# Sort of 100,000 edges: key parts in bf16, interleaved one-hots, and another split of the count's one-hots between VectorE and ScalarE

## What is computed

```python
edge_index = jnp.stack([src, dst])
h = jnp.maximum(_layernorm(x, axis=-1), 0.0)
x = x + _L0_gnn_ref(h, edge_index, ...)      # mean over edges by dst, three layers
h = jnp.maximum(_layernorm(x, axis=-1), 0.0)
x = x + _L1_gnn_ref(h, edge_index, ...)      # attention, sums by src
h = jnp.maximum(_layernorm(x, axis=-1), 0.0)
x = x + _L2_gnn_ref(h, edge_index, ...)      # transformer convolution, sums by dst
h = jnp.maximum(_layernorm(x, axis=-1), 0.0)
x = x + _L3_gnn_ref(h, edge_index, ...)      # attention with edge attributes, sums by src
```

## Time and profile before

| | |
|---|---|
| median of 3 runs | 12631.28 us (12626.98 to 12631.36) |
| the profiled execution | 12619.18 us |
| its span | 12617.4 us |
| PE / PEld busy | 7549.2 us (60%) / 5746.9 us (46%) |
| DVE busy | 7916.2 us (63%) |
| ACT busy | 6282.0 us (50%) |
| POOL busy | 8891.0 us (70%) |

### The profile page before, as it was taken

One profiled execution on the slowest core, in us unless ns is written; L12 is line 12 of the kernel. 1 busy time (PEld: TensorE's weight loads), 2 busy tenths in 40 slices (PEclk: granted clock), 3 DMA queues, 4 the chain that ended last, 5 costly groups with the idle time before them and its releaser, 6 DMA issues. The chain is left out here.

```text
span 12617.4 us, 185971 instructions
## 1 busy us (share of the span) xinstructions
PE 7549.2 (60%) x46394; PEld 5746.9 (46%) x46395; DVE 7916.2 (63%) x21707; ACT 6282.0 (50%) x14083; POOL 8891.0 (70%) x9142
## 2 busy tenths in 40 slices
PE   6666455555551112343666676667666766667998
PEld 5666322232220002333466546663666366645766
DVE  8888666666662224333677767776777677775555
ACT  8333233333333333665566546664666366635666
POOL 0777677767767775777777677776777677766775
PEclk9766677767765555565777787778777877775555
DMA  0000111121121113223444544454444444432223
GB/s 33 2 2 2 31 39 39 39 38 39 39 38 39 40 40 48 54 53 52 132 132 132 118 111 133 131 125 105 132 133 132 96 133 131 133 74 58 72 71 63
DMA packets 820582, 949.30 MB, mean 75 GB/s; under 512 B 481147, under 2 KB 557360, under 8 KB 820156
## 3 DMA queue, kind: packets, MB, share of 16 engines
q0 software_dynamic: 343040, 637.31, 22.0%
q1 hardware_dynamic: 477244, 309.04, 9.2%
HBM read 859.26 MB, written 86.39 MB: 75 GB/s over the span
## 5 line engine op out<-in xcount | busy, mean ns | idle before, releaser
L808 POOL DMA_INDIRECT work<-t,idx x3328 | 3176.7, 955 | 1107.3 <-issue 1014.2
L1658 POOL DMA_INDIRECT work<-t,idx x3328 | 3177.6, 955 | 1024.0 <-issue 1013.4
L820 ACT ACTIVATE work<-iota,loc 128x128 f32<-128x128 f32 (+1 forms) x6672 | 2034.6, 387 | 3253.0 <-DVEq L1110 1921.9
L1113 DVE TENSOR_TENSOR work<-work,ps 128x192 f32 x2496 | 882.8, 354 | 1233.2 <-PE ps L1137 933.6
L1137 PE MATMUL ps<-work 128*128 128x192 bf16 x2496 | 412.7, 305 | 1764.1 <-SPq L815 1702.5
L1753 PE MATMUL ps<-work 128*128 x6784 | 1334.1, 379 | 140.9 <-ACT work L833 81.9
L1753 PEld LDWEIGHTS ps<-work 128*128 128x128 f32 x6784 | 1315.6, 297 | 179.5 <-issue 165.4
L1765 PE MATMUL ps<-work 128*128 128x136 f32 x6656 | 1264.8, 348 | 10.9 <-DVE work L1819 10.1
L600 POOL DMA_INDIRECT tab<-work x784 | 863.1, 1101 | 562.0 <-DVE work L453 315.0
L1137 PEld LDWEIGHTS ps<-work 128*128 128x128 bf16 x2496 | 232.4, 113 | 2077.8 <-issue 1069.8
L728 POOL DMA_INDIRECT tab<-work x784 | 818.7, 1044 | 462.7 <-issue 248.2
(11 more groups left out here) (426 smaller groups left out, 17006.6 us busy)
## 6 DMA issues: line engine op xcount, KB each, us to landing
work<-t,idx POOLq DMA_INDIRECT x7488
node<-pl SPq DMA_DIRECT2D x424, 256.0 KB, 3.4
work<-pl SPq DMA_DIRECT2D x54, 512.0 KB
work<-pl SPq DMA_DIRECT2D x106, 256.0 KB, 3.3
tab<-work POOLq DMA_INDIRECT x1568, 2.1
t<-work SPq DMA_DIRECT2D x196, 128.0 KB, 1.8
x<-work SPq DMA_DIRECT2D x196, 64.0 KB, 1.7
h<-work SPq DMA_DIRECT2D x28, 448.0 KB, 2.6
```

The lines of the kernel that those rows point to most:

```text
L808: pool.indirect_dma_start(X[:, j % 4, n, :], None, table, bass.IndirectOffsetOnAxis(ap=idx[k][:, 8 * j + n:8 * j + n + 1], axis=0)).then_i ...
L820: t = act.activation(P[:, b, n, :], iota[:, :], ACT.Square, scale=-1.0, bias=loc[k][:, bass.ds(a + n, 1)])
L1113: added.on(dve.tensor_tensor(av, av, part(z, n), ALU.add))
L1658: pool.indirect_dma_start(X[:, j % 4, n, M - KD:W], None, table, bass.IndirectOffsetOnAxis(ap=idx[k][:, NT * j + n:NT * j + n + 1], axis=0 ...
```

## The change

The two parts of the keys, `hi` and `lo`, and the row of numbers are kept in bf16; all values are below 256, so they are exact there. The row of numbers is a new tile `twice`, in which each number stands twice side by side (0 0 1 1 2 2 ...). The one-hots of two neighbouring columns are interleaved: entry e of column 2 m stands beside entry e of column 2 m + 1. One comparison still makes 8 one-hots, now with the two keys of a pair of columns repeated as a pair. TensorE reads the one-hot of a column, as weights or as moving operand, with a step of two elements, and so does the multiply of `select`.

In the count, ScalarE makes the low one-hots of k = 1 for the first unit of an iteration alone (u = 0), writing each with a step of two and with the key from a new f32 copy `lof` of the low parts of k = 1; VectorE makes those of u = 1 as well, four comparisons in that unit. TensorE's order stays; in the second unit it waits for VectorE in place of ScalarE.

```diff
-            hi, o = area(o, [EP, 2, ET + 16])
-            lo, o = area(o, [EP, 2, ET + 16])
+            hi, o = area(o, [EP, 2, ET + 16], BF)
+            lo, o = area(o, [EP, 2, ET + 16], BF)
+            lof, o = area(o, [EP, ET])
+            twice, o = area(o, [EP, HR, 2], BF)
...
-            OHh, o = area(o, [EP, 4, 8, HR], BF)
-            OHl, o = area(o, [EP, 4, 8, LC], BF)
+            OHh, o = area(o, [EP, 4, 4 * HR * 2], BF)
+            OHl, o = area(o, [EP, 4, 4 * LC * 2], BF)
+            OHh, OHl = [t.rearrange("p u (m e i) -> p u m e i", m=4, i=2) for t in (OHh, OHl)]
...
             def onehots_high(dve, a, k, u, high):
-                dve.tensor_tensor(OHh[:, 2 * k + u], bc(iota[:, None, 0:HR], [EP, 8, HR]),
-                                  bc(hi[:, k, bass.ds(a, 8)][:, :, None], [EP, 8, HR]), ALU.is_equal).then_inc(high.sem, 1)
+                keys_ = hi[:, k, bass.ds(a, 8)].rearrange("p (m i) -> p m i", i=2)[:, :, None, :]
+                dve.tensor_tensor(OHh[:, 2 * k + u], bc(twice[:, None, :, :], [EP, 4, HR, 2]), bc(keys_, [EP, 4, HR, 2]),
+                                  ALU.is_equal).then_inc(high.sem, 1)
...
             def count(pe, u, k, n):
-                return pe.matmul(R[:, LC * k:LC * k + LC], OHh[:, 2 * k + u, n, :], OHl[:, 2 * k + u, n, :], start=False,
-                                 stop=False, skip_group_check=True)
+                return pe.matmul(R[:, LC * k:LC * k + LC], OHh[:, 2 * k + u, n // 2, :, n % 2],
+                                 OHl[:, 2 * k + u, n // 2, :, n % 2], start=False, stop=False, skip_group_check=True)
...
+                    dve.tensor_copy(twice, bc(iota[:, 0:HR][:, :, None], [EP, HR, 2]))
...
+                    dve.tensor_copy(lof, ki[:, 1, :])
...
                             dve.wait_ge(free.sem, free.up())
-                            dve.sem_inc(freel.sem, 1)
+                            if u == 0:
+                                dve.sem_inc(freel.sem, 1)
                             for k in range(2):
                                 onehots_high(dve, i * 16 + 8 * u, k, u, oh)
-                                if k == 0:
+                                if k == 0 or u:
                                     onehots_low(dve, i * 16 + 8 * u, k, u, ohl)
...
-                        for u in range(2):
-                            act.wait_ge(freel.sem, freel.up())
-                            for n in range(8):
-                                t = act.activation(OHl[:, 2 + u, n, :], iota[:, 0:LC], ACT.Square, scale=-1.0,
-                                                   bias=lo[:, 1, bass.ds(i * 16 + 8 * u + n, 1)])
...
+                        act.wait_ge(freel.sem, freel.up())
+                        for n in range(8):
+                            t = act.activation(OHl[:, 2, n // 2, :, n % 2], iota[:, 0:LC], ACT.Square, scale=-1.0,
+                                               bias=lof[:, bass.ds(i * 16 + n, 1)])
...
-                            pe.wait_ge(ohs.sem, ohs.up())
+                            if u:
+                                pe.wait_ge(ohl.sem, ohl.up())
+                            else:
+                                pe.wait_ge(ohs.sem, ohs.up())
```

More of the change, by code:

```diff
@@ L194, in onehots_high @@
             def onehots_high(dve, a, k, u, high):
-                dve.tensor_tensor(OHh[:, 2 * k + u], bc(iota[:, None, 0:HR], [EP, 8, HR]),
-                                  bc(hi[:, k, bass.ds(a, 8)][:, :, None], [EP, 8, HR]), ALU.is_equal).then_inc(high.sem, 1)
+                keys_ = hi[:, k, bass.ds(a, 8)].rearrange("p (m i) -> p m i", i=2)[:, :, None, :]
+                dve.tensor_tensor(OHh[:, 2 * k + u], bc(twice[:, None, :, :], [EP, 4, HR, 2]), bc(keys_, [EP, 4, HR, 2]),
+                                  ALU.is_equal).then_inc(high.sem, 1)
             def onehots_low(dve, a, k, u, low):
-                dve.tensor_tensor(OHl[:, 2 * k + u], bc(iota[:, None, 0:LC], [EP, 8, LC]),
-                                  bc(lo[:, k, bass.ds(a, 8)][:, :, None], [EP, 8, LC]), ALU.is_equal).then_inc(low.sem, 1)
+                keys_ = lo[:, k, bass.ds(a, 8)].rearrange("p (m i) -> p m i", i=2)[:, :, None, :]
+                dve.tensor_tensor(OHl[:, 2 * k + u], bc(twice[:, None, 0:LC, :], [EP, 4, LC, 2]), bc(keys_, [EP, 4, LC, 2]),
+                                  ALU.is_equal).then_inc(low.sem, 1)
             def count(pe, u, k, n):
-                return pe.matmul(R[:, LC * k:LC * k + LC], OHh[:, 2 * k + u, n, :], OHl[:, 2 * k + u, n, :], start=False,
-                                 stop=False, skip_group_check=True)
+                return pe.matmul(R[:, LC * k:LC * k + LC], OHh[:, 2 * k + u, n // 2, :, n % 2],
+                                 OHl[:, 2 * k + u, n // 2, :, n % 2], start=False, stop=False, skip_group_check=True)
             with ExitStack() as st, nc.Block() as block:
@@ L279, in _ @@
                     with act.Fori(0, ET // 16) as i:
-                        for u in range(2):
-                            act.wait_ge(freel.sem, freel.up())
-                            for n in range(8):
-                                t = act.activation(OHl[:, 2 + u, n, :], iota[:, 0:LC], ACT.Square, scale=-1.0,
-                                                   bias=lo[:, 1, bass.ds(i * 16 + 8 * u + n, 1)])
[L285 to L288, removed]
+                        act.wait_ge(freel.sem, freel.up())
+                        for n in range(8):
+                            t = act.activation(OHl[:, 2, n // 2, :, n % 2], iota[:, 0:LC], ACT.Square, scale=-1.0,
+                                               bias=lof[:, bass.ds(i * 16 + n, 1)])
+                        own.on(t)
+                        act.wait_ge(own.sem, own.c)
+                        ov = OHl[:, 2].rearrange("p m e i -> p (m e i)")
+                        act.activation(ov, ov, ACT.Relu, bias=ones[:, 0:1], scale=-1.0).then_inc(ohs.sem, 1)
                         freel.back(act)
@@ L394, in group_edges @@
             LK = [PS[z][:, 0:4 * LC].rearrange("p (i l) -> p i l", i=4) for z in (4, 5, 6, 5)]
-            OHlv = OHl.rearrange("p (k u) n l -> p u k n l", k=2)
+            OHlv = OHl.rearrange("p (k u) m l i -> p u k m i l", k=2)
             with ExitStack() as st, nc.Block(no_gpsimd_drain=True) as block:
@@ L428, in select @@
                     v.on(dve.tensor_tensor(jv, LK[q].rearrange("p (k m) l -> p k m l", k=2),
-                                           OHlv[:, u, :, 2 * q:2 * q + 2, :], ALU.mult))
+                                           OHlv[:, u, :, q, :, :], ALU.mult))
                     dve.wait_ge(v.sem, v.c)
@@ L495, in turn @@
                     for n in range(8):
-                        t = pe.transpose(BT[k][:, n, :], OHh[:, 2 * k + u, n, :], identb[:, :])
+                        t = pe.transpose(BT[k][:, n, :], OHh[:, 2 * k + u, n // 2, :, n % 2], identb[:, :])
                     t.then_inc(tr.sem, 1)
@@ L532, in column @@
                             pe.matmul(LK[q][:, i, :], ht, Ds[:, m % 2, r], start=False, stop=False)
-                        t = pe.matmul(LK[q][:, i, :], HT[:, u, 4 * q + i, :], OHl[:, 2 * k + u, n, :], start=False, stop=True)
+                        t = pe.matmul(LK[q][:, i, :], HT[:, u, 4 * q + i, :], OHl[:, 2 * k + u, n // 2, :, n % 2], start=False,
+                                      stop=True)
                     if n % 2:
```

## The result

The changed kernel takes 12492.86 us (median of 4 runs, 12488.47 to 12495.15) against 12631.32 us of the kernel before: ratio 0.9889, 95% interval 0.9874 to 0.9903, 138 us less. The forecast was 12498.

A forecast was written before the change was run, and what follows sets the result against it. ScalarE was taken to bound the count and GpSimd the rank stage. Gains of 71 (count), 59 (rank) and 3 us (start) sum to 133, so 12631 - 133 = 12498 us, range 12455 to 12562.

The forecast's parts named there:

- The bound of each stage: Sort: ScalarE bounds the count at 2.66 us a unit; GpSimd's scatters bound the rank stage, VectorE 0.6 us a unit behind.
- 5.40 in the sum: Count, rival with comparisons still at one element a cycle: VectorE needs 5.40 us per 16 columns, 12635 us in all; 8%.
- One-hot length: VectorE's comparisons: high one-hots fall from 968 to 563 ns, low ones from 687 to 422.
- The step that led there: One-hots: 832 elements took 443 ns with 16-bit input, 644 in f32, so 16-bit operands halve the part by element.
- Count: Count stage: the loop through ScalarE's single buffer takes 3.87 us per 16 columns against 5.33, gaining 71.5 us.
- The rival that gave the stepped writes 0.45 us an iteration: Count: ScalarE's writing of every second bf16 costs 22 us, 12520 us in all; 6%.
- TensorE's wait for the Relu: Count, sign in the profile: TensorE still waits for ScalarE's Relu, now once in 16 columns and for longer.
- Rank: Rank stage: shorter one-hots lengthen GpSimd's scatters less, gaining 59 us of 111; ends nothing and all 111.
- the stretching that stays: Rank stage: 52 us of the scatters' 111 us of lengthening remain, the middle of 39 and 66.
- the two laws I gave: Rank stage: lengthening falls with one-hot running time, 0.59, leaving 66 us, or with chance and length both, 0.35, leaving 39.
- Start and set-up: Before the first scatter: 3.5 us gained by shorter one-hots, 0.8 us lost to added copies, net 3.
- Stepped weight loads: TensorE, slower rival: loads at step 2 take twice as long, + 29 us count and + 103 us rank, 12763 us; 4%.

The follow-up runs named there:

- experiment 2: The kernel before with only the new split of the count's one-hots, keys in f32 and not interleaved: 12632.92 us against 12633.03.
- experiment 1: The changed kernel with the old split of the count, ScalarE making the low one-hots of k = 1 in both units: 12560.87 us against 12633.03 of the kernel before.
- experiment 3: The kernel before with keys and row of numbers in bf16 but one-hots not interleaved, old split of the count: 12637.53 us against 12633.03.
- experiment 5: The changed kernel with a unit's last select between its two high one-hots in the rank stage: 12470.23 us against 12628.48 of the kernel before.
- experiment 8: The changed kernel with ScalarE's count set in halves, TensorE starting k = 0 earlier, and a select between the high one-hots: 12432.82 us against 12628.48 of the kernel before.
- experiment 4: The changed kernel with every one-hot comparison of the rank loop preceded by the same comparison into a spare tile: 12564.17 us.

## Why the prediction was right

- **The bound of each stage** was read rightly: experiment 2 shows that relieving ScalarE alone leaves VectorE as the bound, at 5.33 us for 16 columns (5.40 in the sum), experiment 1 that shortening VectorE's work alone leaves ScalarE at its 2.68 us a unit.
- **One-hot length**: 563 and 422 ns forecast, 561 and 422 measured. The step that led there was weak. From rows of one-input operations it laid the halving on the 16 bits; experiment 3 shows 970 ns with 16 bits alone. The Trainium skill (Vector Engine (DVE) Microarchitecture Reference, §5.1) also asks for innermost step 1 and more than one innermost element, and has one element read again and again at one a cycle. The trace agrees: 970 ns with a key repeated innermost, 561 with pairs; which of the two conditions failed is not told apart. Whoever had dropped the pairs on the strength of my rows would have gained nothing.
- **Count**: 3.87 us an iteration forecast, 3.93 measured, 67.4 us gained for 71.5. The round's terms are those of the sum; squares to the end of the Relu took 2.80 for 2.75. What is new in it is ScalarE: from its first square to its Relu 2.08 us for 2.03 in the median. Of these 0.04, half is the stepped write (2.06 in experiment 1, where ScalarE also runs without a pause), the rest the start from a standstill (2.05 in experiment 2, which writes packed). The rival that gave the stepped writes 0.45 us an iteration was some twenty times too dear. TensorE's wait for the Relu became shorter, not longer as I had written: 0.62 us each time for 0.93.
- **Rank**: 59 us forecast, 68 measured; the mis-sized term is the stretching that stays, 44 us for 52. It lies between the two laws I gave (39 and 66), nearer to the product of chance and length. Yet neither factor was the 0.59 that I gave both: the long scatters became 163 for 212 (a factor 0.77), and their mean excess over 958 ns 0.27 us for 0.53 (0.51). That their product is near 0.35 is luck. I also wrote that a hit can't last longer than the instruction; half of those that could ran over into a second one. Nor is the stretching a constant: the same rank code left 44, 42, 34 and 34 us in four kernels that differ only in the count, and experiments 5 and 8 left 21 and 14. How the engines happen to stand to each other is worth 7 to 10 us, which the forecast had no term for.
- **Start and set-up**: 3 forecast, 3.4 measured.
- **Stepped weight loads**, the slower rival, cost nothing: 0.74 us per 8 loads in the earlier trace rows, and in the changed kernel:

```profile
198.00 0.74 PEld L210 LDWEIGHTS ps<-work 128*98 128x98 bf16 x8 [0.49 <-DVE work L200]
```

  The 93 ns a load of my sum (0.74 / 8) are too many: the last load of the row is counted to its end. The starts in the count lie 83 ns apart in the median, in both kernels.

The terms were 4 us too high in the count and 9 too low in the rank stage, which partly cancel: 133 forecast, 138 measured in the medians and 139 in the sort.

## What to carry to other kernels

When an engine is relieved, look for the round behind it: here no engine was busy all the time any more, a single buffer's grant, work and release made 3.93 us, and granting it in halves took 0.5 us more off. Keep VectorE instructions with two SBUF inputs short and apart while GpSimd scatters, since they cost a scatter the time that they still run. Here a comparison in 16 bits cost half the time an element (0.51 ns for 1.03) only with the repeated key in pairs, which the shape in the profile doesn't show; look at the duration.

## What the runs showed of the hardware

- A scatter issued by GpSimd is caught by a comparison with two SBUF inputs that is running 0.13 us after its start (343 of 343 in the two traces of before and after), and goes on when it ends: 0.96 us becomes up to 2.26, and 2.54 in experiment 4. One that begins from 23 ns before to 48 ns after the scatter's start, with no other comparison running before it, doesn't catch it (18 such in experiment 5). The Trainium skill (GPSIMD Engine Reference, Key points) names the contention; the size, and that a second comparison right behind holds it in about half of the cases (49 of 97 before, 33 of 78 after), come from these traces.
- Stepping by two bf16 elements costs TensorE's 98-column weight loads nothing (0.74 us per 8 both ways). With stepped writes ScalarE's squares still start every 239 ns; only the Relu behind a row of 8 comes 0.02 us later, though the mean record grew from 332 to 355 ns (before and experiment 1).
- GpSimd's waits for the loaded pairs fell from 8.5 to 0.6 us, but that is no gain: its "issue" time rose from 238.4 to 246.4, and the two together stayed at 246.9 and 247.0 us (247.0 in experiment 5 too, with 4.3 of waits). The pause of 0.3 us between scatters is there either way.
